# Graph network and routed FFN: rows of the state through VectorE block transposes and a DRAM scratch, the gated update as z*h + (1-z)*n

## The reference, cut to what matters

```python
A = (adj != 0)
h = layernorm(x)
for i in range(3):
    m = h @ weight[i]
    aggr = A^T m                      # sum over neighbours, graph by graph
    gi = aggr @ w_ih.T + b_ih ; gh = h @ w_hh.T + b_hh
    r = sigmoid(i_r + h_r) ; z = sigmoid(i_z + h_z)
    n = tanh(i_n + r * h_n)
    h = (1 - z) * n + z * h
x = x + h
```

## Time and profile before

| | |
|---|---|
| median of 3 runs | 492.29 us |
| span of the profiled execution | 490.1 us (first to last instruction; some 2.2 us lie around it) |
| TensorE matmul busy | 480.0 us, 98% |
| VectorE busy | 370.0 us, 76% |
| ScalarE busy | 334.7 us, 68% |
| GpSimd busy | 376.1 us, 77% |
| the chain that ended last | TensorE 94%, ScalarE 2%, VectorE 2%, GpSimd 1% |
| graph network | from 14.5 us (first fused matmul) to about 283 us |

### The profile page before, as it was taken

One profiled execution on the slowest core, in us unless ns is written; L12 is line 12 of the kernel. 1 busy time (PEld: TensorE's weight loads), 2 busy tenths in 40 slices (PEclk: granted clock), 3 DMA queues, 4 the chain that ended last, 5 costly groups with the idle time before them and its releaser, 6 DMA issues.

```text
span 490.1 us, 10428 instructions
## 1 busy us (share of the span) xinstructions
PE 480.0 (98%) x3247; PEld 401.9 (82%) x3247; DVE 370.0 (76%) x1158; ACT 334.7 (68%) x595; POOL 376.1 (77%) x371
## 2 busy tenths in 40 slices
PE   8999999999999999999999999999999999999994
PEld 4788888888888888888888877777769999999994
DVE  4898678789887898888887798878977555655552
ACT  4886996667976768966787698988763554445531
POOL 5389986789988899979778656777777776377576
PEclk9999999999999999999999999999999999999998
DMA  8889000000000000000000000111353342233110
GB/s 217 234 242 289 0 1 0 1 1 1 1 1 2 0 1 2 0 3 0 1 0 1 0 2 18 59 62 57 110 136 100 119 124 86 71 97 90 33 48 24
DMA packets 37317, 27.38 MB, mean 56 GB/s; under 512 B 6140, under 2 KB 33920, under 8 KB 37264
## 3 DMA queue, kind: packets, MB, share of 16 engines
q1 hardware_dynamic: 31344, 17.40, 12.8%
q0 software_dynamic: 4320, 8.93, 5.2%
q10 hardware_dynamic: 1600, 0.40, 0.4%
HBM read 17.12 MB, written 10.04 MB: 55 GB/s over the span
## 4 chain that ended last, share of the span: by engine, by line
PE 94%; ACT 2%; DVE 2%; POOL 1%; issue 1%; POOLq 0%; DVEq 0%
PE bank L484 20%; PE bank L486 19%; PE bank L485 19%; PE bank L736 13%; PE bank L507 4%; PE bank L531 4%; PE bank L530 4%; PE bank L672 3%; PE bank L722 2%; PE bank L629 1%; PE bank L596 1%; PE bank L537 1%; ACT adj_i L948 1%; PE bank L564 1%; PE bank L569 0%
## 5 line engine op out<-in xcount | busy, mean ns | idle before, releaser
L948 ACT ACTIVATE adj_i<-bank,b1c 128x512 f32<-128x512 f32 (+1 forms) x136 | 91.3, 685 | 72.8 <-PE bank L486 72.3
L375 POOL TENSOR_TENSOR diff<-hT,n_sb 128x512 f32<-128x512 f32 x48 | 77.1, 1607 | 12.0 <-ACT n_sb L834 12.0
L451 POOL DMA_INDIRECT sorted_rows<-xrow,pos x64 | 62.2, 972 | 20.0 <-issue 17.9
L736 PE MATMUL bank<-wd_sb,adj_i 128*128 x568 | 66.7, 275 | 0.0
L377 POOL TENSOR_TENSOR diff<-z_sb,diff 128x512 f32<-128x512 f32 x48 | 63.5, 1323 | 3.8
L736 PEld LDWEIGHTS bank<-wd_sb,adj_i 128*128 128x128 f32 x568 | 65.1, 192 | 0.2
L484 PE MATMUL bank<-ag_hi,wf_hi 128*128 128x512 f32 x144 | 61.0, 424 | 0.0
L484 PE MATMUL bank<-hT_hi,w_hi 128*128 128x512 f32 (+1 forms) x136 | 58.3, 429 | 0.9 <-ACT adj_i L948 0.7
L486 PE MATMUL bank<-ag_hi,wf_lo 128*128 128x512 f32 x144 | 57.1, 397 | 0.0
L485 PE MATMUL bank<-ag_lo,wf_hi 128*128 128x512 f32 x144 | 56.7, 394 | 0.0
L484 PE MATMUL bank<-hT_hi,whh_hi 128*128 128x512 f32 x132 | 54.0, 409 | 0.0
(11 more groups left out here) (185 smaller groups left out, 1158.2 us busy)
## 6 DMA issues: line engine op xcount, KB each, us to landing
adj_i<-sorted_rows SPq DMA_DIRECT2D x71, 72.0 KB
xrow<-in_x_dram SPq DMA_DIRECT2D x16, 256.0 KB, 3.7
adj_i<-in_adj_dram SPq DMA_DIRECT2D x16, 256.0 KB, 4.0
sorted_rows<-xrow,pos POOLq DMA_INDIRECT x64, 2.3
sorted_rows<-padrow SPq DMA_DIRECT2D x9, 72.0 KB
out_dram<-cand,home POOLq DMA_INDIRECT x39
bd_bc<-in_L_ffn_bd_dram SPq DMA_DIRECT2D x1, 512.0 KB, 4.1
out_dram<-n_sb,home POOLq DMA_INDIRECT x32
```

The lines of the kernel that those rows point to most:

```text
L375: nc.gpsimd.tensor_tensor(diff[:, b, :], hT[:, g, :], n_sb[:, b, :], ALU.subtract).then_inc(diff_ok, 1)
L451: nc.gpsimd.indirect_dma_start(out=sorted_rows, out_offset=bass.IndirectOffsetOnAxis(ap=pos[:, g, j:j + 1], axis=0), in_=xrow[:, g * GR + ...
L736: last = nc.tensor.matmul(o, HT[:, sg % 2, k, j * P:(j + 1) * P], wd_sb[:, bass.ds(at + k * P, P)], start=(k == 0), stop=(k == KC - 1))
L948: nc.scalar.activation(HT[:, hb, k, 0:n], HB[k][:, 0:n], ACT.Gelu, bias=b1c[:, k:k + 1]).then_inc(done, 1)
```

## The change

- **Rows of the state.** The four TensorE transposes of the units of layers 1 and 2 go, with the ScalarE and VectorE operations that split them. In their place VectorE turns the 32x32 blocks of the new state (`state_blocks`, one 128x512 instruction from `hT` to `blocks`), and SyncE writes `blocks` to a DRAM tensor `swap` with one DMA, waits for it, and reads it back into `hn` with four DMAs (`state_turned`). This is done for the 32 units of layers 0 and 1 (`TURNED`).
- **Neighbours.** `A`, `xn` and `hn` are plain fp32 there; one matmul for each graph takes the place of the two with the high and the low half. All splits of these rows go, also in layer 0.
- **Update.** ScalarE computes z and, from the same bank, keep = sigmoid(-(.)) = 1-z. GpSimd makes z*h in the same step as the unit (`old_part`), n*keep one step later (`new_part`), and VectorE adds the two one step later (`state(s-1)` where `state(s-2)` stood, and at another place of the list: behind the turned rows, ahead of `reset(s)`).
- **Loads.** SyncE loads groups 0 to 7, then handles 8 turned states, then loads groups 8 to 15, 8 more turned states, the FFN weights, and the rest.

The core of the diff:

```diff
+    swap = nc.dram_tensor("swap", (2, QP, P, P), fp32).ap()
...
+            def state_turned(k):
+                b = k % 2
+                sp.wait_ge(blk_ok, k + 1)
+                hold(sp, hn_in[b], k // 2 * QP * 16)
+                sp.dma_start(swap[b].rearrange("s p e -> p s e"),
+                             blocks[:, b, :].rearrange("p (s e) -> p s e", s=QP)).then_inc(blk_out, 16)
+                sp.wait_ge(blk_out, (k + 1) * 16)
+                if k >= 2:
+                    sp.wait_ge(ag_ps, made("all", TURNED[k - 2] + QUAD))
+                for f in range(QP):
+                    sp.dma_start(hn[:, b, f * P:(f + 1) * P], swap[b, :, f * SUB:(f + 1) * SUB, :]).then_inc(hn_in[b], 16)
...
+            def old_part(u):
+                b = u % 2
+                hold(pool, z_ok, made("all", u))
+                hold(pool, h_ok, made("all", u - 2))
+                nc.gpsimd.tensor_tensor(diff[:, b, :], z_sb[:, b, :], hT[:, u % QUAD, :], ALU.mult).then_inc(zh_ok, 1)
+
+            def new_part(u):
+                b = u % 2
                 hold(pool, n_ok, made("all", u))
...
+                hold(pool, kept_ok, made("all", u))
+                nc.gpsimd.tensor_tensor(n_sb[:, b, :], n_sb[:, b, :], keep[:, b, :], ALU.mult).then_inc(nk_ok, 1)
...
             def step_gnn(s):
-                if first(s + 1):
-                    first_rows_low(s + 1)
                 if exists(s - 1):
-                    old_state(s - 1)
+                    new_part(s - 1)
...
                     state_low(u)
+                if exists(s):
+                    old_part(s)
...
                 else:
-                    hold(pe, hnhi_ok, made("later", u))
-                    hold(pe, hnlo_ok, made("later", u))
...
+                    k = made("later", u) - 1
+                    pe.wait_ge(hn_in[k % 2], (k // 2 + 1) * QP * 16)
+                    rows_of = hn[:, k % 2, :].rearrange("p (c g) -> p g c", g=GR)
...
-                    nc.tensor.matmul(pAG[:, c], hn_hi[:, u % 2, c], A[:, u % QUAD, c], start=True, stop=False)
-                    last = nc.tensor.matmul(pAG[:, c], hn_lo[:, u % 2, c], A[:, u % QUAD, c], start=False, stop=True)
+                    last = nc.tensor.matmul(pAG[:, c], rows_of[:, j], A[:, u % QUAD, c], start=True, stop=True)
...
-                if exists(u):
+                if first(u):
                     unit_turned(u)
...
             def update(u):
                 hold(act, z_ps, made("all", u))
-                nc.scalar.activation(z_sb[:, u % QUAD, :], pZ[:], ACT.Sigmoid, bias=bsum[:, 1:2]).then_inc(z_ok, 1)
+                hold(act, zh_ok, made("all", u - 2))
+                nc.scalar.activation(z_sb[:, u % 2, :], pZ[:], ACT.Sigmoid, bias=bsum[:, 1:2]).then_inc(z_ok, 1)
+                hold(act, nk_ok, made("all", u - 2))
+                nc.scalar.activation(keep[:, u % 2, :], pZ[:], ACT.Sigmoid, bias=bkeep[:, 0:1], scale=-1.0).then_inc(kept_ok, 1)
...
             def state(u):
-                hold(dve, zd_ok, made("all", u))
+                hold(dve, zh_ok, made("all", u))
+                hold(dve, nk_ok, made("all", u))
                 tt(hT[:, u % QUAD, :], n_sb[:, u % 2, :], diff[:, u % 2, :], ALU.add).then_inc(h_ok, 1)
+
+            def state_blocks(u):
+                k = made("inner", u) - 1
+                dve.wait_ge(h_ok, made("all", u))
+                hold(dve, blk_out, (k - 1) * 16)
+                nc.vector.transpose(blocks[:, k % 2, :].rearrange("p (s e g) -> p g s e", g=GR, s=QP),
+                                    hT[:, u % QUAD, :].rearrange("p (g s e) -> p g s e", g=GR, s=QP)).then_inc(blk_ok, 1)
...
-                if exists(s - 2):
-                    state(s - 2)
...
-                if exists(s + 1):
-                    rows_low(s + 1)
+                if first(s + 1):
+                    first_rows_low(s + 1)
                 if s + 1 == UN:
                     turned_low(0)
+                if exists(s - 1):
+                    state(s - 1)
+                    if layer(s - 1) < LAYERS - 1:
+                        state_blocks(s - 1)
                 if exists(s):
                     reset(s)
                     candidate(s)
```

More of the change, by code:

```diff
@@ L252, in build @@
         RETIRE = (6, 12)
-        DVE_LOW = (0, 1, 2, 3)
         ACT_UNITS = 2
+        TURNED = [u for u in range(UN) if layer(u) < LAYERS - 1]
+        FIRST_LOADS = GROUPS // 2
         FFN_WEIGHTS = UN - 9
@@ L295, in _, with load_group @@
             load_adj(1)
-            for g in range(2, GROUPS):
+            def load_group(g):
                 sp.wait_ge(x_in[g % 2], g // 2 * 16)
@@ L308, in _ @@
             sp.dma_start(bg_bc[:], bg.partition_broadcast(P)).then_inc(ffn_in, 16)
+            for k in range(4 * QUAD, len(TURNED)):
+                state_turned(k)
             sp.wait_ge(c_gp, 8)
@@ L498, in unit_turned @@
             def unit_turned(u):
-                if layer(u) == 0:
-                    hold(pe, xn_ok, made("first", u))
-                    src = xn
-                else:
-                    hold(pe, h_ok, made("all", u - 4))
-                    src = hT
+                hold(pe, xn_ok, made("first", u))
                 hold(pe, h0_ok, made("first", u - 1))
                 for j in range(GR):
-                    last = nc.tensor.transpose(pT[:, j * P:(j + 1) * P], src[:, u % QUAD, j * P:(j + 1) * P], ident[:])
+                    last = nc.tensor.transpose(pT[:, j * P:(j + 1) * P], xn[:, u % QUAD, j * P:(j + 1) * P], ident[:])
                 last.then_inc(t_ps, 1)
@@ L918, in step_gnn @@
                     gate_rows((s - GATE_ROWS) // 2, (s - GATE_ROWS) % 2)
[L919 to L924 removed]
+                if first(u):
+                    rows_turned_high(u)
                 if u == UN:
@@ L934, in step_gnn @@
                     state_high(u)
-                if s >= 3 and first(s + ahead(s)[SPLIT]):
-                    rows_high(s + ahead(s)[SPLIT])
                 if s == FFN_WEIGHTS:
```

114 lines of the change are left out of this document (40 added, 74 removed).

## The result

The changed kernel takes **542.38 us** (median of 4 runs, 540.33 to 543.97) beside 492.27 for the kernel before on the same chip: 1.1019 times as long, interval 1.1002 to 1.1036. Measured again later it was 549.83 beside 492.15, 1.1182 (1.1132 to 1.1233). The forecast of 508.1 has the sign right, but the time lies outside the range of 490 to 520. The profiled execution's span went from 490.1 to 540.3: +50.2, where 15.8 was summed up.

What follows compares the result with a forecast made beforehand. TensorE was taken to set the step before, a two-step loop through ScalarE, GpSimd and VectorE after. Seven terms, 0.8+2.5+3.8+3.8+1.3+0.6+3.0 = 15.8, took the span from 490.1 to 505.9, with 2.2 around it 508.1 us; range 490 to 520.

Steps and rivals of the forecast that it cites:

- the two-step loop: Fused matmuls of s to those of s+2, through ScalarE, GpSimd and VectorE: 11.19 us, 5.60 a step against 5.54.
- Costed at nothing. The trip through DRAM: SyncE's write and reads of a turned state: 6 to 7.4 us plus five issues, covered by 10 us.
- Rival 4: DRAM trip outlasts its 10 us, 3.4 late in 8 hops, some 27 us half hidden: about 520; chance 0.06.
- the strided weights: TensorE's neighbour weights read from hn with a stride of four elements: cost from nothing to a doubled load.
- Rival 5: Strided neighbour weights double eight loads, adding 0.9 to 32 short steps: about 515 to 525; chance 0.06.
- the transpose: VectorE's block transpose in the loop: 0.69 us, 0.61 as spacing, bounds 0.53 to 1.2, worth -1 to +7 us.
- the opening: Step 2 gets two transposes and state(1) in VectorE and loses one split, half in waits: +0.8 us.
- the loops of the four passes: Two-step loops plus added statistics, adjacency, row_scale and normalisation: +2.5, +3.8, +3.8 and +1.3 us.
- the two row_scales steps: Steps 24 and 36, row_scales between old_part and new_part in GpSimd: loop of 13.6 against 12.1, +1.5 us each.
- 1 (TensorE stays the bound): The two-step loop comes under 10.34 us and additions find slack, so TensorE sets the step: 481.3 us; chance 0.14.
- 3 (the shared port): GpSimd's row_scale holds VectorE's sum 0.92 us in two loops of three passes: +5.5, 513.6 us; chance 0.05.
- the likeliest case: The two-step loop with its additions takes back TensorE's gain: 508.1 us, 499 to 517 by itself; chance 0.64.

Runs made afterwards that it cites:

- e15: Changed kernel without the DRAM trip (hn filled once), with contiguous neighbour weights and block transposes written as runs of 32 words: 514.14 us beside 492.15.
- e1: Changed kernel without the trip through DRAM, hn filled once from x and never rewritten: 595.39 us, ratio 1.0606 to the kernel before.
- e11: Changed kernel with four writes, one read, a ScalarE gathering copy, four order changes and transposes in runs of 32 words: 562.35 us, ratio 1.0015.
- e16: The e12 kernel measured again in another series: 485.67 us beside 492.15, ratio 0.9866.
- e2: e1 with neighbour weights read as contiguous elements instead of with a stride of four: 589.39 us, ratio 1.0499 to the kernel before.
- experiment 3: Kernel before with only the neighbour sum changed to one plain fp32 matmul per graph: 560.21 us beside 558.76, ratio 1.0022.
- e12: e11 with the first two row_scales batches cut in two and state(1) one step later in the opening: 554.16 us, ratio 0.9868.
- e3_update_alone: e2 with VectorE's 32 block transposes left out too: 576.75 us, ratio 1.0274 to the kernel before.

## Why the prediction was wrong

The +50.2 us, by the steps taken away one at a time in this order (another order would share them out a little differently, since where one wait goes the next one holds):

| part | us | from |
|---|---|---|
| the two-step loop and the update, transpose at 0.71 | 16.8 | e15, before |
| the stride of four words | 10.8 | e1, e15 |
| the trip through DRAM | 17.3 | changed, e1 |
| the turn to the gate | 5.6 | 14.27-8.68 |
| sum | 50.5 | |

The last 0.2 to 0.3 are the stretch behind the first gate matmul (200.3 and not 200.6) and rounding. e15 and e1 each hold one fall of the clock in a row_scales step that the kernel before and the changed kernel don't have; with 1.4 for it, the first part is 15.4 and the trip 18.7.

**The step that failed: "Costed at nothing. The trip through DRAM".** It set the landing of one 256 KB load and one 64 KB transfer against 10 us of cover: "write and reads need 6 to 7.4 plus SyncE's five issues". With the issues at 2.6 that was at its upper end 10.0 already, for a cover of 10, and it should have stood as a bound. Three sizes in it were wrong. The write does not land after 3.7 or 2.3 but after 4.5 to 4.9, where it stands behind the four reads of the state before (2.8 where SyncE had ended their issue 1.4 us earlier, 2.3 with nothing ahead of it); a read in 512-byte pieces lands after 4.2 and not 2.3; so the trip is 10.6. Above all, it asked only how long one state takes, and never how often SyncE can do it: with a wait in its list for each write, SyncE does one state in 7.0 us, and 8 come in a row, one per step. Lateness adds up from state to state. Rival 4 named the place and gave "3.4 late in 8 hops"; its chance of 0.06 rested on "the queue is idle in these steps", which the kernel's own eight states in a row refute. On its own it would have been about 17 (24 in the later run, 332.52 less the 308.38 of e1).

**The second: the strided weights, "the bound is from nothing to a doubled load".** The load takes 0.33 and not 0.19, 1.7 times, and the neighbours 1.66 and not 0.84. Rival 5 had taken +0.9 for the eight; it was +0.82 beside before. It had 0.06. The nothing that was taken had no row for it; the middle of its bounds would have been +0.45 in a step.

**The third: the transpose.** Its estimate of 0.69 had rows of side-by-side words behind it, and where the words are side by side (e11, e15, e16) it is 0.71. The change writes every fourth word, and takes 1.12 a transpose; the forecast saw that stride for the weights and not for this write. 1.12 lies within its bounds of 0.53 to 1.2, which were given "-1 to +7 us"; e2 against e15 is 6.7, with two falls of the clock more in e2. The Trainium skill, "SBUF — State Buffer", section "Door 1: The DMA port swizzle", says that an access that crosses to a new 16-byte line pays a penalty, and four fp32 words are 16 bytes. The trace agrees: 0.33 against 0.19, 1.12 against 0.71, 1.12 against 0.62. The same section gives four fp32 as the stride up to which nothing is paid; here a stride of exactly four paid, and the measurement decides.

**The fourth was not looked at:** the turn from the graph network to the FFN, 5.6 us. The sum moved ahead of everything in VectorE's step, and at the last unit this means ahead of the low half that feeds TensorE, while the tanh on which it depends keeps its late place. 1.4 of the 5.6 is the clock that fell behind TensorE's 4.08 of idle time; no term of the sum had the clock. The question that gives it is what is queued behind each wait that the change adds; it was asked for the steady steps alone.

**What was right.** The sign, and the reason given for it: TensorE's gain is real (no transposes of hT in the short steps, 128 instructions fewer) and a two-step loop through GpSimd and VectorE takes it back. Built by itself, that case measured 16.8 where the sum of seven terms was 15.8. That they come so near is in part luck. Term by term (e15 less before, the forecast in brackets): the opening 2.2 (0.8), the loops of the four passes 2.2, 2.5, 2.8 and 1.7 (2.5, 3.8, 3.8 and 1.3), the two row_scales steps 2.3 and 3.3 (1.5 each; 1.4 of the 3.3 and of the last pass's 1.7 is the clock), the long steps 0 (0.6). Terms too small made up for terms too large. In kind it is the forecast's loop: GpSimd's product releases the sum, and TensorE's idle time is released by VectorE's low half. The two steps with row_scales were put at 13.6, too low: they are 14.5 in the changed kernel, 14.2 and 15.2 in e15, and 13.5 to 15.7 in the others that keep it whole. Plain fp32 was put at +0.06 a step, and is 0.00 (experiment 3). The long steps were put at 6.04, and take 5.97. A short step that TensorE alone bounds was put at 5.17, and is 5.09 to 5.17 in e11, e12 and e16.

**Rivals.** 1 (TensorE stays the bound) is the state of e11 and e12, reached by other orders and by words side by side, and not by this change. 3 (the shared port) may show in two rows, the sums of the two steps with row_scales of the changed kernel (183.36 and 262.56), with low price:

```profile
183.36 1.70 DVE L1133 TENSOR_TENSOR hT<-n_sb,diff 128x512 f32<-128x512 f32 x1 [1.74 <-POOL n_sb L406]
```

1.70 (the other 1.69) and not 0.70, but in the steps with row_scale, where the rival had it, the sum took 0.69 to 0.71. 4 and 5 were both true, at the same time as the likeliest case: they were written as other ways and given 0.06 each, when nothing made them exclude each other or it. Three causes that each lengthen the same step do not have chances that add up to one, and the range should have reached to their sum.

## What to carry to other kernels

A transfer that is made once per step needs two numbers set against the step: how long it takes from issue to landing, and how often its queue can do it, with every wait and issue in that queue's list and with the transfer before it still under way. Before layout is moved from an engine to an access pattern, take the stride in bytes at each place that reads or writes it: words side by side in the buffer and one gathering in an engine with room cost less than a stride that three engines pay for. And follow a moved instruction also in the first and the last steps of its loop, where what stands around it is different.

## What was not expected of the hardware

- The same 256 KB write lands after 2.3 us on an idle queue and after 4.4 to 4.9 right behind four 64 KB reads in 512-byte pieces. These reads move 63 GB/s, the write itself up to 272 (114.0 to 115.0 us), though its pieces have 512 bytes too. As one read in 2 KB pieces the same 256 KB lands after 2.7, at 187 GB/s, and SyncE issues it in 0.34, not 2.2.
- A stride of four fp32 words costs a weight load 1.7 times its time (0.33, 0.19), a VectorE transpose that writes with it 1.6 (1.12, 0.71), and a ScalarE copy that reads with it 1.8 (1.12, 0.62).
- GpSimd's pow of 128x4 takes 1.02 to 1.03, nearly as long as its product of 128x512 (1.24 to 1.31). In e3_update_alone that is enough to make GpSimd's own list the chain of the step.
- TensorE's granted clock fell from 2.4 to 1.2 GHz after idle times of 2.1 us in some executions and not in others (1.4 us lost in a row_scales step), and after those of 4.08 at the gate in the changed kernel. So a wait can cost more than it lasts. What decides between the executions was not found.
- The changed kernel, whose trip is not hidden, differs by 1.4% between two measurements (542.38, 549.83); the kernel before differs by 0.02% between them (492.27, 492.15).
